# Attention and feed-forward as one program: second norm and first gate-and-up blocks between the last tiles' steps

## The chip, the core and the metric

The kernel runs on one core of one Trainium2 chip. The core has a matrix engine (TensorE, PE in the profile; its weight loads are PEld), a vector engine (VectorE, DVE), a scalar engine (ScalarE, ACT), GpSimd (POOL) and SyncE (SP), which here only issues DMAs. Each engine works through its own queue in order and waits on semaphores. The metric is device time in microseconds for one execution; lower is better.

## The reference

One transformer layer over `x` of shape (4, 256, 512): four sequences of 256 tokens, 512 channels.

```
mod = silu(c) @ wmod -> sa, ca, ga, sb, cb, gb     # six rows of 512 for each of the 4 sequences
ga, gb: sign kept, magnitude at least 0.25
h = layernorm(x) * (1 + ca) + sa
q, k, v = h Wq, h Wk, h Wv; rope on q and k         # 32 heads, 8 key heads, head size 128
dt = softplus(h Win + bias); G = cumsum(-dt * exp(A)) in chunks of 128
y = (q k^T * exp(G_i - G_j), lower triangle) (v dt) + (q exp(G)) state of the chunk before
y = y / rms(y) * gnorm * silu(h Wg)
x = x + ga * (y Wo)
h = layernorm(x) * (1 + cb) + sb
x = x + gb * (silu(h Wgate) * (h Wup)) Wdown        # inner width 1376
```

## The kernel before

**Numbers.** Most products are kept near full precision by splitting both operands in a rounded part and a rest (`split_hi`, a cast, L44; `split_lo`, a subtraction, L49) and adding three products (`three_products`, L54 to L56). A block of a projection is 4 slices of the 512 channels times three products: 12 matmuls of 128 x 512 into one PSUM bank. A few products stay in plain float32.

**Three parts, two programs.** `block_attention` does everything up to the residual `x1 = x + ga * attention`; `block_ffn` holds two blocks of its own, gate and up first, down second. Between these three blocks every engine waits for all others. The token axis is 8 tiles of 128 (`t`, two to a sequence) or two halves of 512.

**Prologue of the attention.** The rows `sa` and `ca` come from `mod_row` (L588): 4 matmuls with a stationary operand of 4 columns, added up in PSUM, then copied and turned into columns (`mod_turn`, L597). First norm (`Norm`), first key and value projection, and four steps t = -4 to -1 that project queries (`q_block`) and gates (`g_block`) for the first half. Among them are the softplus chain on VectorE (semaphore `chain`), the cumulated decays (`cumulative`, L626 to L632), their store to DRAM and the broadcast load back into `dec` (`load_dec`, L445), which ScalarE awaits in `exp_g` (L783). GpSimd clears `x1` (L1395) once the first norm has turned its tiles. The loop's first product is `scores` (L670).

**The loop.** `groups` runs 8 groups of 4 heads over 8 tiles. A step holds scores, `q_block` and `g_block` for the next half, `y_product`, `out_product` (12 matmuls, added to `x1` by `add_out` one step later) and `square_sum`. Seven groups are a hardware loop, the last is written out.

**The last four tiles** have no projection left for the next half, so `tail(g, t)` takes the place of `step`. It fills TensorE's queue with the four remaining modulation rows (`mod_row` of GA, CB, GB, SB). VectorE bounds the gates (`guard_gate`), SP stores them, loads them back as broadcast rows (`grow`), loads `x` again, and GpSimd does `scale_tile` and `add_x` (L406, L413) for tiles 0 to 6, VectorE for tile 7. Statistics of the second norm are taken there too (`stats_of`).

**Feed-forward.** After the barrier the second norm is normalised, turned (L165), modulated by ScalarE (L175) and split; 11 slices of 128 inner channels follow, each for two halves: gate block, up block (12 matmuls each), `Silu` on ScalarE (L1561), product on VectorE (L1595), split into `a_hi` and `a_lo`. Gate and up have two PSUM banks each. The weights alternate between two buffers. After the second barrier the down projection takes 8 tiles x 11 slices x 3 matmuls, result scaled by `gb`, added to `x1` and stored.

Of the kernel before, what the change touches and what calls it, by code (L numbers as in the profile page):

```python
# [5 lines left out]
ALU = mybir.AluOpType  # L6
# [4 lines left out]
P = 128  # L11
# [4 lines left out]
EPS = 1e-5  # L16
# [12 lines left out]
POOL_TILES = 7  # L29

# [8 lines left out]
SA, CA, GA, SB, CB, GB = range(6)  # L39

# [18 lines left out]
def build(nc, x_in, cT_in, wmod_in, wq_in, wg_in, wkv_in, wo_in, win_in, rows_in, gnorm_in,  # L59
# [4 lines left out]
    with ExitStack() as outer:  # L64
        def sb(name, shape, dt=F32, side=None):
            return outer.enter_context(nc.sbuf_tensor(name, shape, dt, side=side))
# [13 lines left out]
        block_attention(nc, cst, x1, hT_hi, hT_lo, tok, modT, gnorm, ident, modrow, gT_dram,  # L80
                        x_in, cT_in, wmod_in, wq_in, wg_in, wkv_in, wo_in, win_in, rows_in,
                        gnorm_in, cst_in, wgu_in, norm_rows, raw_pair)
        block_ffn(nc, x1, hT_hi, hT_lo, modT, ident, modrow, wgu_in, wd_in, out, norm_rows,
                  raw_pair)
# [110 lines left out]
def block_attention(nc, cst, x1, hT_hi, hT_lo, tok, modT, gnorm, ident, modrow, gT_dram,  # L195
                    x_in, cT_in, wmod_in, wq_in, wg_in, wkv_in, wo_in, win_in, rows_in,
                    gnorm_in, cst_in, wgu_in, norm_rows, raw_pair):
    with ExitStack() as ctx:
        def sb(name, shape, dt=F32, side=None):
            return ctx.enter_context(nc.sbuf_tensor(name, shape, dt, side=side))  # L200
# [4 lines left out]
        def sem(name):  # L205
# [37 lines left out]
        ps_q, ps_g, ps_kv, ps_s, ps_y, ps_x, ps_ss, ps_o = (  # L243
            ps(n) for n in ("ps_q", "ps_gt", "ps_kv", "ps_s", "ps_y", "ps_x", "ps_ss", "ps_o"))
# [4 lines left out]
        silu_c = sb("silu_c", [P, KT * B])  # L249
# [7 lines left out]
            for i in range(6))  # L257
# [3 lines left out]
        wmod = {SA: qT[:, 1], CA: sg[:, 1]}  # L261
        mod_rows = sg[0:B, 0, 0:2]
        ps_rows = {SA: ps_q[0:B], CA: ps_g[0:B]}
        ps_modT = ps_o[:, 0:2 * KT * B].rearrange("p (m k b) -> p m k b", m=2, k=KT)
        ps_z, ps_glast = (ps_o[:, i * NT * H:(i + 1) * NT * H].rearrange("p (t h) -> p t h", h=H)
                          for i in range(2))
        ps_zT = ps_gT = [ps_x, ps_ss]

        wmod[GA] = raw_o
        wmod[GB] = [raw_kv[:, 0:2].rearrange("p k d -> p (k d)"),  # L270
                    raw_kv[:, 2:4].rearrange("p k d -> p (k d)"),
                    raw_q[:].rearrange("p k d -> p (k d)"), raw_g[:].rearrange("p k d -> p (k d)")]
        wmod[CB], wmod[SB] = qT[:, 0], sg[:, 0]
        late_rows = dec[0:B, 0].rearrange("p h c i -> p (h c i)")\
            .rearrange("p (m n) -> p m n", m=2)
        gates = [q_sin[0:B], tok[0:B].rearrange("p t r h -> p (t r h)")[:, 0:HID]]
        gmag = q_cos[0:B]
        ps_rows.update({GA: ps_q[0:B], GB: ps_g[0:B], SB: ps_kv[0:B], CB: ps_q[0:B]})
        ps_late_modT = ps_q[:, 0:2 * KT * B].rearrange("p (m k b) -> p m k b", m=2, k=KT)
        grow, x_again = raw_o, [qT[:, 0], sg[:, 0]]  # L280
        norm = Norm(ctx, nc, "1", norm_rows, x1, hT_hi, hT_lo, modT[:, 0], modT[:, 1], ident,
                    [ps_s, ps_y, ps_x, ps_ss], True, hf)
        norm2 = Norm(ctx, nc, "2", norm_rows, x1, None, None, None, None, None, None, True, None)
# [71 lines left out]
        small_loaded = sem("small_loaded")  # L355
        sigc_done = sem("sigc_done")
# [16 lines left out]
        gates_ready = sem("gates_ready")  # L373
# [4 lines left out]
        xa_loaded = [sem(f"xa_loaded{i}") for i in range(2)]  # L378
        scaled = [sem(f"scaled_{n}") for n in ("pool", "dve")]
        residual = [sem(f"residual_{n}") for n in ("pool", "dve")]  # L380
        block = ctx.enter_context(nc.Block())
# [10 lines left out]
        def groups(engine, step, tail):  # L392
# [5 lines left out]
            for t in range(NT):  # L398
                if t < 4:
                    step(KVH - 1, t, True, True, False)  # L400
                else:
                    tail(KVH - 1, t)
# [6 lines left out]
        def add_x(engine, queue, who, t, n):  # L409

            queue.wait_ge(scaled[who], n + 1)
            queue.wait_ge(xa_loaded[t // 4], 16)
            engine.tensor_tensor(x1[:, t], x1[:, t], x_again[t // 4][:, t % 4], ALU.add)\  # L413
                .then_inc(residual[who], 1)

        @block.sync
        def _(sp):
            def load_mod(m):
                if m == GB:
                    for k in range(KT):  # L420
                        sp.dma_start(wmod[m][k], wmod_in[m][:, k]).then_inc(mod_loaded[m], 16)
                else:
                    sp.dma_start(wmod[m][:], wmod_in[m]).then_inc(mod_loaded[m], 16)
# [33 lines left out]
            for j in range(1, GRP):  # L457
                load_head(0, j)
# [7 lines left out]
            load_o(0)  # L466

            def step(g, t, project, next_batch, next_group):
# [14 lines left out]
                if not next_group and t == 1:  # L483
                    sp.wait_ge(wo_split, KVH + 1)
                    sp.wait_ge(wo_late, KVH + 1)
                    load_mod(GA)
                    load_mod(GB)

            def tail(g, t):
                if t == 4:  # L490
                    step(g, t, False, True, False)
                    sp.wait_ge(zz_done, g * 8 + 4)
                    load_mod(CB)
                    load_mod(SB)
# [1271 lines left out]
```

## Time and profile before

| | us |
|---|---|
| median of 3 runs (lowest, highest) | 1100.27 (1097.45, 1101.43) |
| the profiled execution, as timed | 1100.45 |
| its span in the trace | 1098.7 |
| TensorE busy / VectorE / ScalarE / GpSimd | 1045.7 / 816.6 / 696.6 / 224.2 |

The profiled execution lies 0.2 us above the median. The span runs from the first to the last instruction; 1.75 us lie around it. Mean granted TensorE clock 0.979. Times below are from the start of the span. A matmul's printed duration covers its way through the array, so that neighbours overlap: what one costs in a row of them is the distance of their starts.

### The profile page before, as it was taken

How to read it: one execution, taken by the hardware profiler on the slowest of the kernel's cores; microseconds unless marked ns; L12 is line 12 of the kernel's file. 1: busy time of each engine (PE TensorE's matmuls, PEld its weight loads, DVE VectorE, ACT ScalarE, POOL GpSimd, SP SyncE). 2: the span in 40 equal slices, each digit the busy share in tenths (PEclk: the TensorE clock that was granted, in tenths of full speed). 3: DMA queues.
4: the chain of work that ended last, by engine and by line, in shares of the span. 5: the costliest groups of instructions: out<-in, count | busy, mean ns of one | idle time of the engine just before them, and what ended most of it. 6: DMA issues, size and time to landing. Idle time of an engine off the chain costs nothing. (4 is left out here: it accounts for less than half of the span.)

```text
span 1098.7 us, 14605 instructions
## 1 busy us (share of the span) xinstructions
PE 1045.7 (95%) x4680; PEld 808.4 (74%) x4680; DVE 816.6 (74%) x1585; ACT 696.6 (63%) x1368; POOL 224.2 (20%) x140
## 2 busy tenths in 40 slices
PE   5879999999999999999999999999997859999898
PEld 1657777777777777877777777787774349888786
DVE  5777887888888788878888887887878785444412
ACT  3448877887787788778878787877874434222300
POOL 3412212222211131122222112211323410000000
PEclk9989999999999999999999999999998969999999
DMA  6122301310131122013101311220123231111011
GB/s 226 55 67 80 112 20 38 100 53 19 38 115 39 33 85 91 19 38 115 38 19 38 126 44 40 77 76 19 45 72 135 76 129 45 57 38 58 29 39 38
DMA packets 37464, 70.89 MB, mean 65 GB/s; under 512 B 2936, under 2 KB 19576, under 8 KB 35520
## 3 DMA queue, kind: packets, MB, share of 16 engines
q1 hardware_dynamic: 36720, 70.16, 19.8%
q10 hardware_dynamic: 720, 0.43, 0.1%
q8 instruction: 13, 0.21, 0.1%
q14 instruction: 11, 0.09, 0.0%
HBM read 68.33 MB, written 2.24 MB: 64 GB/s over the span
## 5 line engine op out<-in xcount | busy, mean ns | idle before, releaser
L1373 POOL TENSOR_TENSOR q_sin<-q_sin,cst 128x512 f32<-128x512 f32 x64 | 88.9, 1388 | 311.7 <-ACT q_sin L764 311.7
L1213 DVE SCALAR_TENSOR_TENSOR prob<-ps_s,scal,dec 128x128 f32<-128x128 f32 x256 | 71.9, 343 | 77.6 <-PE ps_s L670 77.6
L1361 POOL TENSOR_TENSOR dec<-dec,future 128x1024 f32<-128x1024 f32 x31 | 74.5, 2402 | 265.9 <-ACT expg L783 265.9
L54 PE MATMUL ps_q<-hT_hi,wq_hi 128*128 128x512 f32 x256 | 125.5, 490 | 3.3 <-DVE q_cos L1023 2.5
L54 PE MATMUL ps_o<-wo_hi,z_hi 128*128 128x512 f32 x260 | 103.8, 399 | 2.5 <-DVE z_lo L49 2.4
L54 PE MATMUL ps_gt<-hT_hi,wg_hi 128*128 128x512 f32 x256 | 103.8, 405 | 2.0 <-DVE sg L1043 2.0
L56 PE MATMUL ps_o<-wo_hi,z_lo 128*128 128x512 f32 x260 | 103.4, 398 | 0.0
L55 PE MATMUL ps_o<-wo_lo,z_hi 128*128 128x512 f32 x260 | 103.2, 397 | 0.0
L56 PE MATMUL ps_q<-hT_hi,wq_lo 128*128 128x512 f32 x256 | 101.2, 395 | 0.0
L55 PE MATMUL ps_gt<-hT_lo,wg_hi 128*128 128x512 f32 x256 | 101.1, 395 | 0.0
L56 PE MATMUL ps_gt<-hT_hi,wg_lo 128*128 128x512 f32 x256 | 100.7, 393 | 0.0
L55 PE MATMUL ps_q<-hT_lo,wq_hi 128*128 128x512 f32 x256 | 100.4, 392 | 0.0
L805 ACT ACTIVATE sq_parts<-sq_sum 64x512 fp32r<-64x512 f32 x64 | 40.5, 633 | 65.9 <-DVE sq_sum L1232 64.3
L793 ACT ACTIVATE dec<-dec,scal 128x128 f32<-128x128 f32 x256 | 81.1, 389 | 1.3 <-DVE scal L994 1.3
L54 PE MATMUL ps_kv<-wkv_hi,hT_hi 128*128 128x256 f32 x256 | 73.1, 286 | 0.0
L55 PE MATMUL ps_kv<-wkv_lo,hT_hi 128*128 128x256 f32 x256 | 72.7, 284 | 0.0
L56 PE MATMUL ps_kv<-wkv_hi,hT_lo 128*128 128x256 f32 x256 | 72.7, 284 | 0.0
L54 PEld LDWEIGHTS ps_q<-hT_hi,wq_hi 128*128 128x128 f32 x256 | 48.5, 190 | 27.0 <-issue 17.0
L670 PE MATMUL ps_s<-qT,kT 128*128 128x512 f32 x128 | 65.8, 595 | 2.5 <-DVE qT L1031 2.5
L55 PEld LDWEIGHTS ps_q<-hT_lo,wq_hi 128*128 128x128 f32 x256 | 48.6, 190 | 22.5 <-issue 14.4
L773 ACT ACTIVATE sig<-sig 128x512 f32<-128x512 f32 x64 | 39.9, 624 | 35.9 <-DVE sig L1037 35.5
L1043 DVE SCALAR_TENSOR_TENSOR sg<-ps_gt,gnorm,sig 128x512 f32<-128x512 f32 x64 | 47.9, 748 | 18.3 <-ACT sig L775 18.2
(251 smaller groups left out, 2737.6 us busy)
## 6 DMA issues: line engine op xcount, KB each, us to landing
dec<-gT_dram SPq DMA_DIRECT2D x32, 512.0 KB, 5.5
raw_q<-wq_in SPq DMA_DIRECT2D x32, 256.0 KB, 2.7
raw_g<-wg_in SPq DMA_DIRECT2D x32, 256.0 KB, 2.9
raw_o<-wo_in SPq DMA_DIRECT2D x8, 1024.0 KB, 6.9
raw_pair<-wkv_in SPq DMA_DIRECT2D x8, 512.0 KB, 4.7
raw_pair<-wgu_in SPq DMA_DIRECT2D x6, 512.0 KB, 3.2
raw_gu<-wgu_in SPq DMA_DIRECT2D x5, 512.0 KB, 3.4
qT<-wmod_in SPq DMA_DIRECT2D x2, 1024.0 KB, 6.9
```

Of the source, the lines that this page charges most:

```text
L54: pe.matmul(out, w_hi, x_hi, start=first, stop=False)
L55: pe.matmul(out, w_hi, x_lo, start=False, stop=False)
L56: return pe.matmul(out, w_lo, x_hi, start=False, stop=last)
L670: nc.tensor.matmul(ps_s[:].rearrange("p (h i) -> p h i", h=GRP), kT[:, b % 2, c * P:(c + 1) * P], qT[:, half, :, rows_of(t)], start=True, ...
L773: nc.scalar.activation(sig[:], sig[:], ACT.Ln, bias=1.0).then_inc(lsig_done, 1)
L793: last = nc.scalar.activation(cell, cell, ACT.Exp, bias=scal[:, bn * CPB + c, 0, h:h + 1])
L805: nc.scalar.activation(sq_parts[0:64], sq_sum[:], ACT.Copy).then_inc(sqhi_done, 1)
L1043: nc.vector.scalar_tensor_tensor(sg[:, half, j], ps_g[:], gnorm[:], sig[:], ALU.mult, ALU.mult).then_inc(sg_done, 1)
L1213: last = nc.vector.scalar_tensor_tensor(prob[:, h], ps_s[:, h * P:(h + 1) * P], scal[:, tile, 1, h:h + 1], dec[:, tile // 2 % 2, h, tile % ...
L1361: nc.gpsimd.tensor_tensor(cells, cells, future[:].unsqueeze(1).broadcast_to([P, GRP * CPB, CHUNK]), ALU.add).then_inc(mask_done, 1)
L1373: nc.gpsimd.tensor_tensor(q2, q2, sinT, ALU.mult).then_inc(qsin_done, 1)
```

## The change

- One program, one block: `layer` takes the place of `block_attention` and `block_ffn`. The feed-forward's buffers are laid over attention buffers that are free by then.
- **Modulation rows**: all six are computed in the prologue. `silu_c` is padded from 4 to 32 columns, and the four matmuls of a row go to four strips of 32 PSUM partitions (`ps_rows[m][k * LANE:(k + 1) * LANE]`) instead of being added up; `mod_turn` adds the strips by 4 small matmuls with a 0/1 matrix `sel`. ScalarE copies each row out of PSUM (128 x 512). The gates are bounded on 128 x 32 elements in column form (`guard_gates`) and stored to `modrow` by two DMAs of 2048 single float32 each, on SP's queue after `load_o(0)`. The clearing of `x1` moves to t = -2.
- **Last four tiles**: `tail` is gone. A list written out by hand for each engine holds their steps, the second norm in five sets of tiles (`LN_SETS`), and the gate and up blocks e = 0, 1, 2 of the feed-forward. For these three ScalarE makes the sigmoid from exp, log and exp. The squares are taken whole and summed by a plain float32 product. `residual_tile` on GpSimd starts with tiles 0 and 1 in steps 2 and 3 of the last group.
- **Feed-forward**: the first two slices are loaded and split twice, once for each half (13 weight loads for 22 blocks). Gate and up have one PSUM bank each. ScalarE does all hi splits of the weights, GpSimd the first three lo splits, VectorE the others. The down projection begins without a barrier; ten of its weight slices' loads are spread over the last blocks.

```diff
-C_ID, C_COST, C_SINT, C_COS, C_SIN, C_TRI, C_END = 0, 128, 384, 640, 896, 1152, 1280
+C_ID, C_COST, C_SINT, C_COS, C_SIN, C_TRI, C_SEL, C_END = 0, 128, 384, 640, 896, 1152, 1280, 1288
+LANE = 32
+FIRST_W = 2
+W_ORDER = list(range(IT)) + list(range(FIRST_W))
+FFN = [(i, it, half) for i, it in enumerate(W_ORDER)
+       for half in ((0,) if i < FIRST_W else (1,) if i >= IT else (0, 1))]
+LN_SETS = ((0, 2), (2, 2), (4, 2), (6, 1), (7, 1))
...
+            def mod_rows(m):
+                pe.wait_ge(mod_loaded[m], 16)
                 for k in range(KT):
+                    nc.tensor.matmul(ps_rows[m][k * LANE:(k + 1) * LANE], silu_c[:, k], wmod[m][:, k],
+                                     start=True, stop=True).then_inc(rows_ready, 1)
...
+            sp.wait_ge(guard, GUARD_END)
+            for i in range(2):
+                sp.dma_start(modrow[i].rearrange("(m p) -> p m", p=P),
+                             gate_T[:, i].rearrange("p b k -> p (b k)"),
+                             allow_slow_non_contiguous=True).then_inc(rows_stored, 16)
...
             softplus_argument()
+            pe.wait_ge(norm.hf_done, NT)
+            mod_rows(GA)
             q_block(0, -3)
             softplus_turn()
+            pe.wait_ge(kT_done, 1)
+            mod_rows(GB)
             g_block(0, -3, 0, KT)
+            mod_turn(2)
+            mod_rows(SB)
             q_block(0, -2)
+            mod_turn(3)
+            mod_rows(CB)
             g_block(0, -2, 0, KT)
             cumulative()
+            mod_turn(4)
             q_block(0, -1)
+            mod_turn(5)
             g_block(0, -1, 0, KT)
+            pe.wait_ge(late_modT_done, 2)
...
+            scores(g, 4)
+            cross_scores(g, 4)
+            kv_chunk(g, 2, 0)
+            kv_chunk(g, 2, 1)
+            y_product(g, 4)
+            scores(g, 5)
+            out_product(g, 4)
+            square_sum_whole(g, 4)
+            y_product(g, 5)
+            ln_turn(0)
+            square_sum_whole(g, 5)
+            k_turn(g, 2)
+            scores(g, 6)
+            cross_scores(g, 6)
+            out_product(g, 5)
+            ln_turn(1)
+            scores(g, 7)
+            y_product(g, 6)
+            out_product(g, 6)
+            square_sum_whole(g, 6)
+            y_product(g, 7)
+            ffn_gate(0)
+            ffn_up(0)
+            square_sum_whole(g, 7)
+            out_product(g, 7)
+            ffn_gate(1)
+            out_product(g, 8)
+            ffn_up(1)
+            ln_turn(2)
+            ln_turn(3)
+            ffn_gate(2)
+            ln_turn(4)
+            ffn_up(2)
+            for e in range(EARLY_E, len(FFN)):
+                ffn_gate(e)
+                ffn_up(e)
+            pe.wait_ge(alo_done, len(FFN))
...
+            for e in range(EARLY_E, len(FFN)):
+                ffn_prod(e)
+                if e > EARLY_E and e == LAST_OF[i - 1] + 1 and i + 1 < len(W_ORDER):
+                    split_w_lo(i + 1)
+                ffn_lo(e)
```

TensorE's list stands in the first part, VectorE's loop over the later blocks in the last. VectorE's list between `gate(g, 3)` and `y_product(g, 5)`'s last operand is: `ln_stats(0)`, `gate(g, 3)`, `ln_stats(1)`, `gate_y(g, 4)`, `ln_variance(0)`, `probabilities(g, 5)`, `add_out(g, 4)`, `cross_probabilities(g, 4)`, `split_prob_lo(g, 5)`, `ln_normalise(0)`, `split_v_lo(g, 2)`. GpSimd's list there is `residual_tile(2)`, `split_w_lo(0)`, `residual_tile(3)`, `mask`, `split_w_lo(1)`, `ln_lo(0)`, `residual_tile(4)`, `ln_lo(1)`, `residual_tile(5)`, `split_w_lo(2)`, `residual_tile(6)`. ScalarE's begins `split_w_hi(0)`, `copy_v`, `decays(g, 5)`, `squares_whole(g, 4)`, `ln_rstd(0)`, `split_w_hi(1)`.

## Rows read from the trace of the kernel before

**Rows 1.** The page, busy time, share of the span, instructions of each engine

```profile
PE 1045.7 (95%) x4680; PEld 808.4 (74%) x4680; DVE 816.6 (74%) x1585; ACT 696.6 (63%) x1368; POOL 224.2 (20%) x140
```

**Rows 2.** Stretches: length, busy PE, PEld, DVE, ACT, POOL, granted clock, DMA

```profile
46.98:78.58 31.60, 24.58 (x100) 18.21 (x100) 22.90 (x43) 13.82 (x26) 3.84 (x3) 0.89 0.18 54
78.58:827.66 749.08, 749.08 (x3421) 587.10 (x3422) 625.79 (x1270) 593.75 (x1157) 173.41 (x98) 1.00 0.19 60
827.66:904.89 77.23, 55.36 (x179) 28.98 (x178) 61.03 (x111) 31.59 (x70) 25.26 (x16) 0.83 0.32 113
904.89:1028.99 124.10, 124.09 (x590) 105.05 (x588) 54.28 (x75) 33.70 (x60) 0.00 (x0) 0.98 0.15 49
```

**Rows 3.** Who waited for whom, PE, 827.66 to 904.89: total, times, longest

```profile
PE ps_ss L701 <- DVE sq_parts L49: 5.6, 3, 2.5
PE ps_ln L165 <- DVE xn2b L153: 4.7, 1, 4.7
```

**Rows 4.** Timeline of PE: start, duration; one modulation row, then starts of neighbouring blocks

```profile
860.53 3.60 PE L588 MATMUL ps_kv<-sg,silu_c 128*4 128x512 f32 x8
...
865.57 1.02 PE L693 MATMUL ps_x<-qT,kT 128*128 128x512 f32 x2
...
1023.38 0.39 PE L54 MATMUL ps_fg<-hT_hi,wgu_hi 128*128 128x512 f32 x1
...
1026.10 0.39 PE L54 MATMUL ps_fu<-hT_hi,wgu_hi 128*128 128x512 f32 x1
```

**Rows 5.** Groups between 827.66 and 904.89: count, busy, mean ns of one

```profile
L1213 DVE SCALAR_TENSOR_TENSOR prob<-ps_s,scal,dec 128x128 f32<-128x128 f32 x16 | 4.5, 343 | 1.1 <-PE ps_s L670 1.1
...
L124 DVE BATCH_NORM_STATS2 stats<-x 128x6 f32<-128x512 f32 x8 | 5.4, 675 | 0.0
...
L406 POOL TENSOR_TENSOR x<-x,raw_o 128x512 f32<-128x512 f32 x7 | 10.0, 1446 | 21.9 <-DVE x L1049 21.9
```

**Rows 6.** Timeline of DVE and POOL, a cast beside GpSimd's mask and one alone

```profile
843.07 2.34 POOL L1361 TENSOR_TENSOR dec<-dec,future 128x1024 f32<-128x1024 f32 x1 [18.67 <-ACT expg L783]
843.42 2.28 DVE L44 CAST prob_hi<-prob 128x512 fp32r<-128x512 f32 x1
...
871.98 0.43 DVE L44 CAST prob_hi<-prob 128x512 fp32r<-128x512 f32 x1
```

**Rows 7.** VectorE's operations on `wgu_lo`: count, duration in ns min/median/max, first and last start

```profile
L49 DVE TENSOR_TENSOR wgu_lo<-raw_gu,wgu_hi x5: 1224/1225/1226, 916.3 to 999.4; 128x1024 fp32r<-128x1024 f32 x5
```

**Rows 8.** Timeline, the second barrier: VectorE's last steps, TensorE's first

```profile
1029.09 0.69 DVE L1595 TENSOR_TENSOR prod<-ps_fu,prod 128x512 f32<-128x512 f32 x1 [3.36 <-PE ps_fu L56]
...
1030.48 0.69 DVE L49 TENSOR_TENSOR a_lo<-prod,a_hi 128x512 fp32r<-128x512 f32 x1 [0.69 <-ACT a_hi L1564]
...
1032.54 0.62 PE L54 MATMUL ps_d<-d_hi,a_hi 128*128 128x512 f32 x1 [3.56 <-PEq L1446]
```

**Rows 9.** Timeline of the prologue's last steps, all engines

```profile
41.46 3.52 POOL L1395 MEMSET x<- 128x4096 f32 x1
...
56.05 0.47 PE L54 MATMUL ps_q<-hT_hi,wq_hi 128*128 128x512 f32 x1 [2.47 <-DVE q_cos L1023]
...
62.67 0.50 PE L54 MATMUL ps_gt<-hT_hi,wg_hi 128*128 128x512 f32 x1 [2.05 <-DVE sg L1043]
...
70.59 0.39 SPq L445 DMA_DIRECT2D dec<-gT_dram  x1
...
75.34 0.63 ACT L783 ACTIVATE expg<-dec 128x512 f32<-128x512 f32 x1 [0.40 <-DMA dec<-gT_dram]
...
78.58 1.13 PE L670 MATMUL ps_s<-qT,kT 128*128 128x512 f32 x2 [2.51 <-DVE qT L1031]
```

**Rows 10.** The page's DMA queues: packets, MB, share of 16 engines' span

```profile
q1 hardware_dynamic: 36720, 70.16, 19.8%
q10 hardware_dynamic: 720, 0.43, 0.1%
```

**Rows 11.** Timeline of ACT: the first `exp_g` of the loop

```profile
95.86 0.61 ACT L783 ACTIVATE expg<-dec 128x512 f32<-128x512 f32 x1
```

More of the change, by code:

```diff
@@ L1 @@
+import math
 from contextlib import ExitStack
@@ L273, in block_attention @@
[L273 to L280, printed above, removed]
+        ps_zT = ps_gT = [ps_x, ps_ss[:]]
@@ L390, in group_slice, with groups @@
             return bass.ds(g * size, size)
-        def groups(engine, step, tail):
+        def groups(engine, step, between):
             with engine.Fori(0, KVH - 1) as g:
@@ L397, in groups @@
                     step(g, t, True, True, True)
[L398 to L402, printed above, removed]
+            for t in range(4):
+                step(KVH - 1, t, True, True, False)
+                between(t)
         def scale_sum(engine, who, t):
@@ L753, in _, with square_sum_whole, ln_turn @@
-            groups(pe, step, tail)
-            out_product(KVH - 1, NT)
+            def square_sum_whole(g, t):
+                pe.wait_ge(sq_done, g * 8 + (t + 1))
+                pe.wait_ge(lnss_done, g * 8 + t)
+                nc.tensor.matmul(ps_ss[:], ones[:].bitcast(F32), sq_whole[:], start=True, stop=True)\
+                    .then_inc(ss_ready, 1)
+            def ln_turn(s):
+                first, count = LN_SETS[s]
+                pe.wait_ge(xn2_done, first + count)
+                if s == 1:
+                    pe.wait_ge(hf2_done, 1)
+                bank = (pairs[0], pairs[0], pairs[1], ps_s[:].unsqueeze(1), ps_y[:].unsqueeze(1))[s]
+                for c in range(count):
+                    for k in range(KT):
+                        last = nc.tensor.transpose(bank[:, c, k * P:(k + 1) * P],
+                                                   xn2[:, (first + c) % 4, k * P:(k + 1) * P], ident)
+                last.then_inc(turned2, 1)
@@ new lines, in _ @@
+            groups(act, step, lambda t: None)
+            g = KVH - 1
+            split_w_hi(0)
+            copy_v(g, 2)
+            decays(g, 5)
+            squares_whole(g, 4)
+            ln_rstd(0)
+            split_w_hi(1)
+            split_prob_hi(g, 5)
+            inverse_rms(g, 4)
+            exp_g(g, 2)
+            squares_whole(g, 5)
+            ln_modulate(0)
+            copy_kT(g, 2)
+            act.wait_ge(o_ready, g * 8 + 5)
+            split_z_hi(g, 4)
+            ln_rstd(1)
@@ L957, in _ @@
+            act.wait_ge(up_ready, len(FFN))
+            for k in range(D_FIRST, IT):
+                split_d_hi(k)
         @block.vector
@@ L1706, in constants, with between @@
+            def between(t):
+                if t in (2, 3):
+                    residual_tile(t - 2)
+            groups(pool, step, between)
+            residual_tile(2)
+            split_w_lo(0)
+            residual_tile(3)
+            mask(KVH - 1, 2)
+            split_w_lo(1)
+            ln_lo(0)
+            residual_tile(4)
+            ln_lo(1)
+            residual_tile(5)
+            split_w_lo(2)
+            residual_tile(6)
 def constants():
```

1008 lines of the change are left out of this document (538 added, 470 removed).

## The prediction

> **What bounds the kernel now.** The page comes first: TensorE is busy 1045.7 of 1098.7 us, VectorE 816.6 [rows 1]. So a gain of more than a few us must come from the 53 us in which TensorE stands, or from its slow clock. The stretches say where those lie [rows 2]. In the loop (78.58 to 827.66) TensorE is busy in all 749.08 us: nothing there is touched. Between 827.66, where the tail's first `scores` starts, and 904.89, the first gate matmul, 77.23 us pass with 55.36 busy, 21.9 idle, at a mean granted clock of 0.83, a mixture of the two levels (2.4 and 1.2 GHz). The waits there [rows 3] name VectorE's short steps and the normalising behind the barrier: a chain from tile to tile with nothing to fill it. The gate and up stretch, 904.89 to 1028.99, is full again. In the prologue's last part (46.98 to 78.58) TensorE idles 7.0 us.
>
> **The tail before, in full-clock work.** One block of 12 matmuls takes 1026.10 - 1023.38 = 2.72 us, a pair of gate and up 5.44, all 22 pairs 119.7 [rows 4]. As they end at 1028.99, the tail costs 1028.99 - 827.66 - 119.7 = 81.6 us. TensorE's own work in it, from the starts in the timeline at full clock: 4 modulation rows of 3.45 (13.8) and their turns (0.6); 5 out products of 2.8 (14.0); 6 plain float32 products for scores and cross scores of 0.86 [rows 4] (5.2); 4 y products (4.5); one key and value batch (2.9); squares and key turns (1.2); the norm's turns (3.6). Together 45.8. With 21.9 idle, 13.9 are left: what the low clock cost.
>
> **The tail after.** The rows go (-14.4); the square sums become plain float32, 4 x (0.86 - 0.23) = +2.5. So 33.9 of own work, plus 16.3 for three pairs of gate and up. What waits remain I worked out by laying the four lists on one time axis from `scores(g, 4)`, each operation at its duration in the rows (four `probabilities` of 343 ns spaced 0.28 = 1.12, statistics of a tile 0.84, GpSimd's product or addition 1.3 to 1.45 [rows 5]). Of these waits, 18.5 us in all, 12.6 come in three places:
> - before `y_product(g, 5)`, 6.4. VectorE reaches `gate_y(g, 4)` at 9.2, since ScalarE does `split_w_hi(0)`, `copy_v` and `decays(g, 5)` before the squares; then probabilities, `add_out`, cross probabilities, rest of prob (13.7), `ln_normalise(0)` (16.0) and `split_v_lo` stand before it, to 16.3. TensorE had run out at 10.1.
> - before `out_product(g, 5)`, 3.6: `z_lo` is behind statistics of two tiles, a split and GpSimd's `ln_lo(0)`; it ends at 26.5.
> - before gate e = 3, 2.6: the third sigmoid by exp, log and exp comes after the last modulations, and frees the single gate bank late.
>
> The rest: 1.5 (set 3 to be normalised), 1.4 and 1.2 (before `y_product(g, 7)` and `out_product(g, 6)`), 1.1 (`kT`), 0.7 in small ones. Gate 3 starts at 33.9 + 16.3 + 18.5 = 68.7, against 81.6 + 16.3 = 97.9 before: **-29.2**. VectorE has about 47 us of work in these 68 and GpSimd 35, so they are nearly as loaded as TensorE: these waits are VectorE's order, not slack.
>
> In that axis a VectorE operation between SBUF tensors waits for GpSimd's running one, and the reverse. The row that shows it: a cast of 0.43 us alone takes 2.28 when it starts in GpSimd's mask, and ends with it [rows 6]. If they ran side by side unhindered, gate 3 would start at 60.1. The Trainium skill (SBUF — State Buffer, Terms, "shared port pair") says that the loser "fully blocks" for the whole instruction; by that rule, which speaks against moving norm work and residuals beside VectorE, and with which the row agrees, it is 68.7.
>
> **The low clock.** It cost 13.9 before with 21.9 idle; with 18.5 idle there are bounds of 0 and 11.7. Doubling TensorE's operations in the 14 us behind the first wait and the 10 us behind the second moves gate 3 by 3.9, as VectorE covers the rest: **+3.9**, the middle.
>
> **Later blocks.** With one bank each, gate e + 1 needs `Silu` of e (0.6 us, while the up block of 2.7 runs) and up e + 1 the product (0.65, while the next gate runs): covered by 2 us each. The three doubled matters are ACT's hi splits (1.04) and VectorE's rests, 1.23 each [rows 7], for 13 weights instead of 11; ACT and DVE were 34 and 54 of 124 us busy there [rows 2]. One is not covered: e = 20 is a slice with one block only; VectorE does `ffn_prod(20)`, then the rest for slice 12, which gate 21 needs: 0.65 + 1.23 + 0.4 of handing over = **+2.3**. The down projection: before, product, hi, rest and barrier held TensorE 3.56 us, then 8 matmuls at 1.2 GHz (+1.6) [rows 8]; now product, hi and rest alone, 2.4: **-2.8**. If the clock falls in these two gaps, up to 1.6 comes back each. SP's d loads are issued tens of us ahead; if not, TensorE would wait there for one of 2 to 3 us.
>
> **Prologue.** Four more rows stand in TensorE's list. The nearest row prices one at 3.45 [rows 4], whatever the stationary's width. On the timeline: GA from 46.3 to 49.8, `q_block(-3)` to 52.5 (before: 49.9), GB to 56.4, gate block 59.1, SB 62.7, `q_block(-2)` 65.4, CB 68.9, gate block 71.6, then `cumulative`. So TensorE itself, not VectorE, sets that pace, and the idle 2.47 and 2.05 [rows 9] are used up. Behind it the chain is as before: G's store, its load at 70.59, ScalarE's exp at 75.34 when it lands, `scores` at 78.58 [rows 9]. The copy of G could start at 68.3 before and at about 72.8 to 73 now: with late `modT` +0.5, **+5.1**. The other bound: four matmuls in the time of one, 0.86 + 0.15 each. Then `q_block(-2)` starts about when VectorE lets it, as before, and only the extra copies (ACT 4 x 0.6), the bounding of the gates (VectorE 5 x 0.2) and the last wait remain: +0.7. I take the upper, the row's own price. Clearing `x1` (3.52 [rows 9]) moves within the same stretch, and blocks VectorE there instead of at 42: 0 (-1.5 to +2). The first norm: TensorE's turns wait for `modT`, but VectorE takes up the first split only 0.2 us after it could: **+0.3**. `residual_tile` 0 and 1 in steps 2 and 3 of the last group: 6 us of GpSimd beside VectorE, which has 16% of each step free: **+0.5**.
>
> **The stores of the gates.** 4096 packets of 4 bytes stand in SP's queue before the `dec` load of the loop's first step. 256 per DMA engine: at the packet time of ScalarE's queue, 0.1% x 16 x 1098.7 / 720 = 24 ns, 6 us; at that of q1, whose packets hold 1.9 KB, 19.8% x 16 x 1098.7 / 36720 = 95 ns, 24 us [rows 10]. Issued at 82.9 and behind `wo` (4.8), the `dec` load (5.3) then lands at 99 or 117; ScalarE wants it at 95.86 + 5.1 = 101 [rows 11]. So 0 or +16; the packet is nearer to the small ones: 0.
>
> **Sum.** 1100.45 - 29.2 + 3.9 + 2.3 - 2.8 + 5.1 + 0.3 + 0.5 = 1080.6. The profiled execution stands 0.2 above the median.
>
> **Rivals.**
> - *Rows side by side* (33%). The same chain with the prologue's other bound: 1080.6 - 4.4 = 1076.2; with a mild clock, 1072. For it: the change gives each matmul its own strip of 32 partitions and its own start and stop, and nothing else. Against: no row shows two matmuls at once; a 4-column operand costs as much as a 128-column one. The Trainium skill (TensorEngine Tiling (Array Packing), Performance Considerations) says that a stationary side of 32 or less can be tiled 4 times by columns. By that rule the later four rows take 4 us of TensorE instead of 13.8.
> - *The tail's order is worse than laid out* (15%). In-order lists with hand-set order lose where one step is late: each lateness of VectorE is paid by TensorE. If idle and low clock stay as before (21.9 + 13.9 instead of 18.5 + 3.9), it gives +13.4: 1094; half of it 1087.
> - *The stores hold back `dec`* (5%), the case that ends on the other side: if a 4-byte write takes 0.15 us, 256 of them take 38, `dec` lands at 131, ScalarE stands 30 us in the first step and TensorE with it, since scores of the third tile need `dec`: 1111. It decides from 0.12 us per packet.
> - *The change does not do what it says*: it does by its lists; only the three pairs' place could be worthless if VectorE were the bound throughout (3%): 1100.
>
> **How the numbers follow.** The forecast has 44%. The range holds it with the first rival and the half of the second: 1069 (side by side, clock at its lower bound, 1076.2 - 3.9 = 1072.3, and the freed 3 us at 42) to 1090. Left out are the other half of the second rival, the stores and the last, near 16%. About 0.5% (5.5 us) can be told from no change. Faster by more: all but the stores, the last, and a sliver of the second: 0.92; within: 0.04; slower: 0.04.
>
> **What would show it.** Gate matmuls of e = 3 begin 65 to 73 us after the last group's fifth `scores`, with the longest waits before `y_product(g, 5)` (on VectorE), `out_product(g, 5)` and gate 3. Two gaps of 2.3 us stand before gate 21 and before the down projection. Strip matmuls in the prologue follow one another if serial, and run in the same stretch if not; the loop begins at 83 to 84 or at 79. TensorE busy stays near 1045 - 14 x (side by side) + 2.5. The forecast is wrong if the tail's idle is above 22 us, if ScalarE waits for a DMA at the first `exp_g`, or if the stretch of later blocks isn't full.

## The result, and the profile after

The changed kernel takes 1087.95 us (median of 4 runs, 1087.06 to 1089.31), the kernel before 1099.13 (4 runs of the same measurement). The ratio is 0.990, 95% interval 0.987 to 0.992: 1.0% less time. The predicted 1080.6 is 7.4 us too low; the range, 1069 to 1090, holds the result. The profiled execution took 1087.06 us with a span of 1085.3, against 1100.45 and 1098.7 before: 13.4 less on both counts. When the changed kernel ran again, one of its four executions took 2660.7 us, like no other here; the median given for it below is that of the other three.

The page's first part, beside [rows 1]: TensorE has 8.0 us less work and stands only 47.6 us.

```profile
PE 1037.7 (96%) x4668; PEld 809.6 (75%) x4668; DVE 794.3 (73%) x1556; ACT 707.9 (65%) x1381; POOL 234.9 (22%) x145
```

Stretches of the changed kernel answer to [rows 2]: the loop with steps 0 to 3 of the last group, from there to gate 3, on to the down projection, and to the end. Columns: stretch and length; busy PE, PEld, DVE, ACT, POOL with counts; granted clock; DMA share, GB/s.

```profile
83.37:843.46 760.09, 753.09 (x3421) 588.89 (x3422) 627.56 (x1269) 593.33 (x1155) 178.56 (x102) 0.99 0.20 60
843.46:909.21 65.75, 56.70 (x228) 39.20 (x226) 55.32 (x106) 40.50 (x86) 30.76 (x16) 0.94 0.29 92
909.21:1020.60 111.39, 107.12 (x457) 87.74 (x457) 39.78 (x54) 36.05 (x54) 0.00 (x0) 0.97 0.15 48
1020.60:1085.30 64.70, 60.52 (x264) 49.41 (x264) 15.73 (x24) 3.38 (x7) 0.00 (x0) 0.99 0.09 33
```

In the kernel before, the down projection starts at 1032.54 [rows 8], and gate 3 would start at 827.66 + 97.9 = 925.56 by the prediction's own count. That gives five parts:

| part | before | after | change | forecast |
|---|---|---|---|---|
| start to the loop's first scores | 78.58 | 83.37 | +4.8 | +5.4 |
| loop and the last group's steps 0 to 3 | 749.08 | 760.09 | +11.0 | +0.5 |
| `scores(g, 4)` to gate 3 | 97.9 | 65.75 | -32.1 | -25.3 |
| gate 3 to the down projection | 106.98 | 111.39 | +4.4 | +1.1 |
| down projection to the end | 66.16 | 64.70 | -1.5 | -1.6 |

The forecast's -2.8 for the down projection is split here: 3.56 - 2.4 = 1.2 lie ahead of it, and the 1.6 of low clock behind its start. The tail gave 6.8 more than forecast. Three other parts took 20 us back, where 7 had been forecast. The largest loss lies in the loop, whose own code hardly changed.

What TensorE waited for in the whole changed kernel (waits on whom: us in total, times, longest), those of the start, of the first norm and those under 2.0 left out:

```profile
PE ps_ss L820 <- DVE sq_parts L63: 7.0, 2, 3.6
...
PE ps_kv_x L731 <- issue: 3.1, 1, 3.1
PE ps_q_gt L858 <- DVE xn L1646: 2.9, 1, 2.9
PE ps_s L68 <- DVE a_lo L63: 2.2, 1, 2.2
PE ps_q_gt L68 <- DVE raw_q L1676: 2.2, 1, 2.2
PE ps_q_gt L68 <- issue: 2.0, 1, 2.0
PE ps_s L789 <- DVE modT L1427: 2.0, 1, 2.0
```

The first row is the one to see: 7.0 us before two square sums, at 113.66 in the loop and at 842.89 in the last group's step 3. [Rows 3] had that pair of names in the tail; now it stands in steps that were full before. Each of the rows got an experiment, or a reading below, but for the last: it stands before the first `scores`, was 2.51 in the kernel before [rows 9], and is 1.9 to 2.0 in the trace of every run below.

### The profile page after: what moved, and what is told of

It is laid out like the page before. It is cut to its first block, busy times and chain, and to the rows that moved or that the text cites. A ratio compares the mean times of both kernels' runs of the same rounds, so it can differ in the third digit from the quotient of the medians.

```text
span 1085.3 us, 14475 instructions
## 1 busy us (share of the span) xinstructions
PE 1037.7 (96%) x4668; PEld 809.6 (75%) x4668; DVE 794.3 (73%) x1556; ACT 707.9 (65%) x1381; POOL 234.9 (22%) x145
## 3 DMA queue, kind: packets, MB, share of 16 engines
HBM read 69.38 MB, written 2.24 MB: 66 GB/s over the span
## 4 chain that ended last, share of the span: by engine, by line
PE 84%; issue 5%; POOL 3%; DVE 3%; DMA 3%; ACT 1%; SPq 1%; POOLq 0%; DVEq 0%; ACTq 0%
PE ps_q_gt L68 13%; PE ps_q_gt L70 13%; PE ps_q_gt L69 13%; PE ps_o L70 5%; PE ps_o L69 5%; PE ps_o L68 5%; PE ps_s L789 5%; PE ps_kv_x L70 3%; PE ps_kv_x L69 3%; PE ps_kv_x L68 3%; PE ps_kv_x L812 2%; PE ps_y L798 2%; DMA dec<-gT_dram 2%; PE ps_ss L820 1%; PE ps_y L806 1%
## 5 line engine op out<-in xcount | busy, mean ns | idle before, releaser
L68 PE MATMUL ps_q_gt<-hT_hi,wq_hi 128*128 128x512 f32 x256 | 126.3, 493 | 0.0
L68 PE MATMUL ps_q_gt<-hT_hi,wg_hi 128*128 128x512 f32 x256 | 103.2, 403 | 0.0
L70 PE MATMUL ps_q_gt<-hT_hi,wq_lo 128*128 128x512 f32 x256 | 100.8, 394 | 0.0
L69 PE MATMUL ps_q_gt<-hT_lo,wg_hi 128*128 128x512 f32 x256 | 100.6, 393 | 0.0
L69 PE MATMUL ps_q_gt<-hT_lo,wq_hi 128*128 128x512 f32 x256 | 100.4, 392 | 0.0
L70 PE MATMUL ps_q_gt<-hT_hi,wg_lo 128*128 128x512 f32 x256 | 100.1, 391 | 0.0
L68 PE MATMUL ps_q_gt<-hT_hi,wgu_hi 128*128 128x512 f32 x176 | 70.3, 400 | 4.3 <-DVE raw_q L1676 2.2
L68 PE MATMUL ps_kv_x<-wkv_hi,hT_hi 128*128 128x256 f32 x256 | 74.4, 291 | 0.0
L69 PE MATMUL ps_kv_x<-wkv_lo,hT_hi 128*128 128x256 f32 x256 | 73.5, 287 | 0.0
L70 PE MATMUL ps_kv_x<-wkv_hi,hT_lo 128*128 128x256 f32 x256 | 73.4, 287 | 0.0
```

The lines of the kernel that those rows point to most:

```text
L68: pe.matmul(out, w_hi, x_hi, start=first, stop=False)
L69: pe.matmul(out, w_hi, x_lo, start=False, stop=False)
L70: return pe.matmul(out, w_lo, x_hi, start=False, stop=last)
```

## The experiments

Ten runs followed: the first four of the table on one chip, the next four on a second, the last two on a third. Medians are compared with the changed kernel's 1088.0 (1087.95); against the 1087.26 that it took when it ran again, on the first four's chip, each gain is 0.7 smaller and each loss 0.7 larger. Each ratio is to the kernel before on the same chip, with its 95% interval.

| run | us | ratio to before |
|---|---|---|
| changed kernel, again | 1087.26 | 0.988 (0.985 to 0.990) |
| gate_rows | 1080.13 | 0.981 (0.978 to 0.983) |
| residual_later | 1083.87 | 0.985 (0.983 to 0.986) |
| clear_later | 1083.89 | 0.985 (0.983 to 0.986) |
| rows_in_turn | 1093.27 | 0.994 (0.992 to 0.996) |
| pairs_behind | 1096.90 | 0.997 (0.995 to 0.998) |
| w12_first | 1085.34 | 0.987 (0.986 to 0.989) |
| gate2_silu | 1085.54 | 0.988 (0.986 to 0.990) |
| three_cures | 1074.35 | 0.977 (0.975 to 0.980) |
| all_cures | 1068.77 | 0.973 (0.970 to 0.975) |

**The mark, the changed kernel again.**

> The changed kernel once more, as the mark that the other three of this set are read against. Every theory: 0.99 of the kernel before, near 1088 us.

It came out at 0.988, 1087.26 us. Its trace shows how far two executions of one kernel differ: the first `scores` comes at 81.98 in place of 83.37, since the clock did not fall behind the wait before the cumulative sum (3.06 there, 3.10 in the changed kernel's trace), and the wait before the square sum in the loop is 5.41 us in place of 3.63.

**gate_rows: the stores of the gates.**

```diff
-            sp.wait_ge(guard, GUARD_END)
-            for i in range(2):
-                sp.dma_start(modrow[i].rearrange("(m p) -> p m", p=P),
-                             gate_T[:, i].rearrange("p b k -> p (b k)"),
-                             allow_slow_non_contiguous=True).then_inc(rows_stored, 16)
+            sp.wait_ge(gates_copied, 1)
+            sp.dma_start(modrow.rearrange("i (m p) -> (i m) p", p=P), gate_rows[:]).then_inc(rows_stored, 16)
...
+            nc.tensor.transpose(ps_ss[0:2 * B * KT, 0:P], gate_T[:].rearrange("p m b k -> p (m b k)"),
+                                ident).then_inc(gates_turned, 1)
```

> The gate vectors leave as 32 rows of 512 bytes in one transfer, turned on TensorE and copied out of a PSUM bank that is free by then, in place of 4096 elements of 4 bytes in two. Theory: the small elements hold the queue, so the decay of the next batch lands late, the exp of decay waits 4.3 us for it, and TensorE waits 3.6 us before the square sum of step 0 and runs at the low clock behind that. Without them both go: 3 to 6 us less than the changed kernel, and scores(0,0) to scores(7,4) 755 us in place of 760. Rival: the first steps are late because the prologue leaves TensorE at the low clock and VectorE with a backlog, and the transfers only look long: under 1.5 us less, and the wait before the square sum of step 0 stays over 2.5 us.

Measured: 7.9 us less (7.1 against the repetition), more than expected. SyncE's queue (start, duration of the issue) in the changed kernel, then in this one:

```profile
82.18 4.32 SPq L555 DMA_DIRECT2D modrow<-gate_T  x2
86.88 0.55 SPq L524 DMA_DIRECT2D dec<-gT_dram  x1
87.69 1.69 SPq L507 DMA_DIRECT2D raw_q<-wq_in  x1
89.48 8.36 SPq L509 DMA_DIRECT2D raw_g<-wg_in  x1
```

```profile
81.50 0.43 SPq L557 DMA_DIRECT2D modrow<-gate_rows  x1
85.90 0.40 SPq L527 DMA_DIRECT2D dec<-gT_dram  x1
86.56 0.35 SPq L510 DMA_DIRECT2D raw_q<-wq_in  x1
87.01 0.38 SPq L512 DMA_DIRECT2D raw_g<-wg_in  x1
```

Two issues of 4-byte elements hold SyncE 4.32 us. The last line's issue, 8.36 here, takes 7.5 to 9.7 in four of the eight traces with these stores, and 0.38 in the other four, so it isn't what costs. The `dec` load is issued 4.7 us behind the start of the stores, and in gate_rows 4.4: the held queue isn't it either. From issue to landing, the changed kernel's table of transfers (last column, us) reads, and below it that of gate_rows:

```profile
dec<-gT_dram SPq DMA_DIRECT2D x1, 512.0 KB, 19.7
...
modrow<-gate_T SPq DMA_DIRECT2D x2, 8.0 KB, 17.2
```

```profile
dec<-gT_dram SPq DMA_DIRECT2D x1, 512.0 KB, 5.6
```

So it is the landing: `dec` lands at 86.88 + 19.7 = 106.6, and ScalarE, which takes it at 101.64 in gate_rows, stands 4.3 us for it. ScalarE's exp of the decay and its copy for the square sum, then TensorE's square sum, in the changed kernel:

```profile
106.73 0.63 ACT L983 ACTIVATE expg<-dec 128x512 f32<-128x512 f32 x1 [4.32 <-DMA dec<-gT_dram]
```

```profile
113.66 0.47 PE L820 MATMUL ps_ss<-sq_parts,ones_r 128*128 128x512 f32 x1 [3.63 <-DVE sq_parts L63]
113.97 1.24 PE L789 MATMUL ps_s<-qT,kT 128*128 128x512 f32 x2
115.00 1.92 PE L812 MATMUL ps_kv_x<-qT,kT 128*128 128x512 f32 x2
```

The last line takes 1.92 us where it takes 1.02 in gate_rows: the clock fell to its lower level behind the wait (granted clock 0.84 in 109:120, 1.00 in gate_rows). The stretch 100:120 in the changed kernel, and in gate_rows:

```profile
100.00:120.00 20.00, 16.37 (x60) 11.53 (x60) 15.36 (x30) 12.38 (x24) 3.90 (x3) 0.91 0.32 87
```

```profile
100.00:120.00 20.00, 20.00 (x84) 15.34 (x84) 18.55 (x38) 16.85 (x34) 5.15 (x3) 1.00 0.32 105
```

Full, and at clock 1.00. The rival asked for a wait still over 2.5 us; none is left. From the first `scores` to the last group's fifth it is 754.34 us in place of 760.09, as expected (755). That is 5.8; the medians' 7.9 fits a wait that is longer in other executions (3.3 to 7.7 us in the eight traces with these stores). Two things set it. `dec` lands 19.3 to 22.1 us after its issue. And ScalarE comes to it 19.0 us behind the first `scores` where the clock fell there (the product behind it takes 1.9 us), 17.3 where it didn't (1.02). The four traces with 19.0 have waits of 3.3, 3.6, 3.8 and 5.6 us, the four with 17.3 have 5.3, 5.4, 7.3 and 7.7, each four in the order of the landing. Why the landing varies stays open.

**residual_later: two residual tiles on GpSimd.**

```diff
-                if t in (2, 3):
-                    residual_tile(t - 2)
+                if t == 3:
+                    residual_tile(0)
+                    residual_tile(1)
```

> Residual tiles 0 and 1 both go behind step 3 on the POOL queue, in place of one behind step 2 and one behind step 3. Theory: residual tile 0 holds the rotation q_sin on POOL for 3.2 us, so the q add of the last projection is late and TensorE idles 3.4 us at 842.9 and runs at the low clock behind it: that goes, 3 to 6 us less than the changed kernel. Rival: TensorE waits there for something that comes late anyway (the scores of step 4 need the same kT and the same VectorE queue), or the wait returns one step further, where POOL now does two tiles together: within 1.5 us of the changed kernel.

Measured: 4.2 us less (3.4 against the repetition). Its four executions all lie below the repetition's three (1080.2 to 1084.7 against 1086.3 to 1088.8), though the intervals of the ratios touch. GpSimd's timeline in the changed kernel:

```profile
834.86 1.48 POOL L487 TENSOR_TENSOR x<-x,raw_o 128x512 f32<-128x512 f32 x1
836.41 1.63 POOL L494 TENSOR_TENSOR x<-x,raw_q 128x512 f32<-128x512 f32 x1
838.00 1.29 POOL L1811 TENSOR_TENSOR q_sin<-q_sin,cst 128x512 f32<-128x512 f32 x1
```

VectorE's, behind it, and TensorE's, behind that:

```profile
839.40 1.67 DVE L1346 TENSOR_TENSOR qT<-q_cos,q_sin 128x512 f32<-128x512 f32 x1 [2.52 <-POOL q_sin L1811]
```

```profile
842.89 0.77 PE L820 MATMUL ps_ss<-sq_parts,ones_r 128*128 128x512 f32 x1 [3.37 <-DVE sq_parts L63]
```

The residual tile stands in GpSimd's order ahead of a rotation that is on the path. With the tiles behind step 3, the rotation starts at 832.23, the q addition at 834.18, TensorE's square sum follows without a wait, and `scores` of steps 3 and 4 lie 837.01 - 825.83 = 11.18 us apart in place of 15.00. Part of it returns, as the rival said: a wait of 1.8 us opens within a `y_product`, and the tail takes 66.94 in place of 65.75. By the starts that leaves 3.8 - 1.2 = 2.6. The profiled execution, 1080.19, is the fastest of the four by 3.5 us.

**clear_later: the memset of `x1`.**

```diff
                     pool.wait_ge(rows_ready, KT * len(MODS))
+                    pool.wait_ge(guard, GUARD_END)
```

> The memset of x on POOL waits for the guarded gates, so it no longer stands beside the end of the softplus series on VectorE. Theory: the memset holds the one VectorE operation that took 2.48 us in place of 0.43 and two more at 1.2 to 1.9, and TensorE waits 3.1 us for their result before the cumulative sum: 2 to 3 us less than the changed kernel, first scores at 81 us in place of 83.4. Rival: the memset only moves and holds VectorE's dec mask and the q add of the last block instead (at 76 to 82 us), or what the cumulative sum gains is waited for again at the dec load: within 1 us, and first scores at 83 us.

Measured: 4.1 us less (3.4 against the repetition; here too no execution overlaps, and the intervals touch), more than expected. GpSimd's memset and VectorE's step beside it in the changed kernel, then VectorE's same step here:

```profile
64.46 3.52 POOL L1834 MEMSET x<- 128x4096 f32 x1
```

```profile
65.64 2.48 DVE L1403 TENSOR_SCALAR raw_o<-raw_o 128x256 f32<-128x256 f32 x1
```

```profile
65.12 0.29 DVE L1403 TENSOR_SCALAR raw_o<-raw_o 128x256 f32<-128x256 f32 x1
```

An operation of 0.29 us takes 2.48 and ends as the memset ends (68.12 and 67.98), on the chain for which TensorE's cumulative sum waits. That wait shrinks from 3.1 to 0.9, and the first `scores` comes at 79.73 in place of 83.37. Of these 3.6 us, 2.2 are the wait, 0.5 were there before it, and most of the rest is the clock, which in the changed kernel's trace fell behind the wait (granted clock of 60 to 79.7: 0.91 there, 1.00 here; the second cumulative product takes 1.86 us there, 1.06 here). It didn't fall in every trace: the seven with this wait have their first `scores` at 81.98 to 83.37, so the edit is worth 2.3 to 3.6 there. It is [rows 6] again, though not every operation is held: one of 128x256 on `raw_o` that starts at 65.30, inside the memset, takes 0.43 us, as it does alone (0.42 in this run).

**rows_in_turn: modulation rows one after the other.**

```diff
-                    nc.tensor.matmul(ps_rows[m][k * LANE:(k + 1) * LANE], silu_c[:, k], wmod[m][:, k],
-                                     start=True, stop=True).then_inc(rows_ready, 1)
+                    nc.tensor.matmul(ps_rows[m][0:LANE], silu_c[:, k], wmod[m][:, k],
+                                     start=k == 0, stop=k == KT - 1).then_inc(rows_ready, 1)
```

> The modulation rows' matmuls all accumulate into the lowest strip of 32 partitions, one after the other, as in the kernel before; the rest of the changed kernel stays (the turning takes that strip alone). Theory: side by side the four matmuls of a row cost about 1.0 us and in turn 3.45 us, so GA, GB, SB and CB, which now stand among the projections, cost 2.4 us more each: 5 to 10 us more than the changed kernel, less what the 3.1 us wait before the cumulative sum takes up. Rival: the prologue is paced by the transfers of the modulation weights and by VectorE's chain, so TensorE's rows are hidden either way: under 2 us more.

Measured: 5.2 us more (6.0 against the repetition), at the low end of what was expected. The edit also puts `sa` and `ca`, at the start, in turn. Its turns of a row read 32 partitions in place of 128, and take 1.05 us each where the changed kernel's take 0.95 to 1.05. TensorE's timeline (start, duration): one row in the changed kernel, and the same row in turn:

```profile
52.46 1.06 PE L694 MATMUL ps_kv_x<-sg,cross 128*32 128x512 f32 x8
```

```profile
54.66 3.62 PE L694 MATMUL ps_kv_x<-sg,cross 128*32 128x512 f32 x8
```

The four strips do run side by side, and the row is done 3.4 times as fast. Four later rows cost 10.2 us more in turn; TensorE is then busy without a break from 46.98 to 86, the wait before the cumulative sum is gone, and the first `scores` comes at 89.07, 5.7 later.

**pairs_behind: the three gate and up pairs.** They stand behind `ln_turn(4)` on TensorE, and their exp, sigmoid, product and split steps behind the norm's on the other engines; two hi splits of weights move with them on ScalarE, and GpSimd's last lo split goes behind its last residual tile.

```diff
-            ffn_gate(0)
-            ffn_up(0)
             square_sum_whole(g, 7)
             out_product(g, 7)
-            ffn_gate(1)
             out_product(g, 8)
-            ffn_up(1)
             ln_turn(2)
             ln_turn(3)
-            ffn_gate(2)
             ln_turn(4)
-            ffn_up(2)
+            for e in range(EARLY_E):
+                ffn_gate(e)
+                ffn_up(e)
```

> The first three pairs of gate and up blocks stand behind the last turn of the second norm's first half, with their steps on ScalarE and VectorE behind the norm's; the norm's steps stay among the last tiles' steps. Theory: the pairs are what TensorE does while the last tiles' chain (squares, inverse rms, z) runs on ScalarE and VectorE; without them these waits open again: 8 to 16 us more than the changed kernel, at 1096 to 1104 us, and the clock of the stretch from scores(7,4) to gate 3 falls under 0.9. Rival: the early norm alone brought the gain and the pairs only move work from behind the stretch into it: within 3 us of the changed kernel.

Measured: 8.9 us more, which leaves a gain of 0.3% over the kernel before. Gate 3 starts at 923.10, 76.67 us behind `scores(g, 4)` in place of 65.75. TensorE's timeline shows what opened:

```profile
886.43 2.07 PE L846 MATMUL ps_ss<-sq_whole,ones_r 128*128 128x512 f32 x2 [2.38 <-ACT sq_whole L1146]
...
893.34 0.47 PE L68 MATMUL ps_o<-wo_hi,z_hi 128*128 128x512 f32 x1 [1.54 <-DVE z_lo L63]
...
899.42 0.90 PE L858 MATMUL ps_s<-cst,xn 128*128 128x128 f32 x4 [2.18 <-DVE xn L1643]
901.50 1.11 PE L858 MATMUL ps_y<-cst,xn 128*128 128x128 f32 x4 [1.19 <-DVE xn L1643]
...
910.54 0.47 PE L68 MATMUL ps_q_gt<-hT_hi,wgu_hi 128*128 128x512 f32 x1 [0.58 <-DVE raw_q L1673]
```

The clock up to the first gate matmul (846.43 to 902.27) is 0.87. The pairs are the filling, and 8.9 of the net 11.2 us hang on them. In the stretch itself they are 10.9 of the 32.1 us: the other 21 remain without them, and come with the rows moved out (14.4 of TensorE's work by the prediction's count) and the norm set among the steps, which no run here takes apart.

**w12_first: the last slice's split.**

```diff
+                if i + 1 == len(W_ORDER) - 1:
+                    split_w_lo(i + 1)
                 ffn_prod(e)
```

and the same for `split_w_hi` ahead of `ffn_silu`.

> The split of the thirteenth slice of the gate and up weights stands ahead of silu(20) and prod(20) on ScalarE and VectorE, in place of behind them. Theory: TensorE's 2.0 us wait before gate 21 at 1011.05 is the low half of that split, late by its place in VectorE's order, and the low clock of the next blocks (0.82 in 1011:1020.6) is set off by it: 2 to 4 us less than the changed kernel. Rival: the wait for prod(20) behind it (2.2 us before down at 1020.6) only grows by what is gained: within 1 us.

Measured: 2.7 us less by the medians; the intervals of the two ratios overlap, so the runs alone don't tell it from nothing. The trace does: the wait of 2.03 before gate 21 is gone, and from gate 3 to the down projection it is 1017.38 - 909.87 = 107.51 us in place of 111.39. TensorE's two waits in the changed kernel, and the one left:

```profile
1011.05 0.47 PE L68 MATMUL ps_q_gt<-hT_hi,wgu_hi 128*128 128x512 f32 x1 [2.03 <-issue]
1020.60 0.50 PE L68 MATMUL ps_s<-d_hi,a_hi 128*128 128x512 f32 x1 [2.24 <-DVE a_lo L63]
```

```profile
1017.38 0.50 PE L68 MATMUL ps_s<-d_hi,a_hi 128*128 128x512 f32 x1 [2.24 <-DVE a_lo L63]
```

A wait of 2.03 cost 3.9: the clock does the rest (0.82 in 1011.05:1020.60 of the changed kernel). From gate 21 to the down projection it is 9.6 us in eight of the nine traces with this wait, and 8.0 in pairs_behind, where the clock did not fall behind it. In this run the wait behind the stores was 7.7 us, which may hide part of the gain in the time.

**gate2_silu: the third pair by Silu, and one turn moved.**

```diff
-            ln_turn(0)
             square_sum_whole(g, 5)
+            ln_turn(0)
...
-            ffn_exp(2)
+            ffn_silu(2)
             ln_modulate(4)
             split_w_hi(3)
-            ffn_sigmoid(2)
```

(with `ffn_cap(2)` and `ffn_gated(2)` left off VectorE's list).

> Two small edits. The third pair's activation is one Silu on ScalarE in place of exp, cap and sigmoid steps through VectorE, and the square sum of tile 5 stands ahead of the norm's turn 0 on TensorE. Theory: TensorE waits 2.2 us before gate 3 for VectorE's product of the second pair, held by the cap and gated steps of the third, and 2.9 us before turn 0 on VectorE's normalised row, which the square sum can fill in part: 2 to 4 us less than the changed kernel. Rival: VectorE is the bound of this stretch whatever the order, and the Silu's table load on ScalarE costs as much as it saves: within 1 us.

Measured: 2.5 us less by the medians, again within the intervals. The wait before turn 0 falls from 2.87 to 1.07, but 0.69 opens before the square sum in front of it and 0.72 before the key turn behind it; that before gate 3 falls only from 2.23 to 1.83, now on the norm's own `hT_lo`. So VectorE's norm steps are nearly as late as the third pair's. `scores(g, 4)` to gate 3 takes 64.53 in place of 65.75, and 0.8 of these 1.2 us lie ahead of the edit, in the first `scores` at a better clock. Neither theory nor rival is shown.

**three_cures and all_cures.** The edits that gained, together: first gate_rows, residual_later and clear_later, then with w12_first and both edits of gate2_silu.

> The gate vectors stored as rows of 512 bytes, residual tiles 0 and 1 behind step 3, and the memset of x behind the gates, together. Theory: the three waits lie in three places (before the first scores, before the square sum of step 0, before the scores of step 3 of the last group), so their gains (0.7, 0.4 and 0.4% of the time, measured alone) add: 14 to 17 us less than the changed kernel, 1071 to 1074 us. Rival: they share one cover, the clock and VectorE's backlog at the loop's start, and two of them together give little more than the larger: 1077 us or more.

> The same three, and the thirteenth slice's split ahead of silu(20), the third pair by one Silu, and the square sum of tile 5 ahead of turn 0. Theory: two more places behind the others, each 2 to 3 us alone: 4 to 6 us less than with the first three, 1066 to 1070 us. Rival: with the earlier waits gone the stretch of the last tiles is bound by VectorE and the later edits give under 2 us more: 1070 us or more.

Measured: 1074.35 and 1068.77. The single gains of the three are 7.9 + 4.2 + 4.1 = 16.2 (13.9 against the repetition), and together 13.7 less than 1088.0, just short of the expected 14 to 17: they nearly add, and the rival's 1077 or more didn't come. The other edits bring 5.6 more, near the sum of their two medians (2.7 and 2.5). In the two traces 3.9 of it is gate 21's wait with the clock behind it, and 1.1 lies in the tail. Against the kernel before it is 2.7% in place of 1.0%. The stretch from the first `scores` to the last group's fifth, in all_cures:

```profile
80.12:829.12 749.00, 749.00 (x3421) 587.09 (x3422) 625.69 (x1269) 592.94 (x1155) 176.48 (x100) 1.00 0.20 61
```

It is full, and as long as before the change (749.08 [rows 2]). So the loop's +11.0 was its two waits and the low clock, behind them and behind the first `scores`.

## Why the prediction was right in range and 7 us off

The measured parts miss their forecasts by -0.6, +10.5, -6.8, +3.3 and +0.1 us in the order of the table. That they sum to 6.5 is in good part luck: the loop's loss and the tail's gain were both missed, with opposite signs.

- **The tail** (-29.2 + 3.9): right in kind, too small. By the timeline, TensorE idles 9.05 us between `scores(g, 4)` and gate 3, where I had 18.5. It is busy 56.7, where I had 50.2 of work and 3.9 for the low clock. The mean granted clock of 0.94 means, by my estimate, 0.12 of the 65.75 us at the lower level, and half of that lost: 3.9, as forecast; so the work itself was 2.6 too small in my count. The step that failed is the wait of 6.4 before `y_product(g, 5)`: I had put `split_v_lo` ahead of it, which makes the values of the next batch and isn't needed there. Measured are 1.05 before it, and 2.87 before the norm's first turn behind it. The 3.6 before `out_product(g, 5)` didn't come. The 2.6 before gate 3 did: 2.2. pairs_behind confirms that the pairs fill waits, for a third of the stretch's gain.
- **The stores of the gates** (0, bounds 0 and +16): the failed step that cost most. Of the two packet times I took the lower. By my own sum (issue at 82.2, `wo` 4.8, `dec` 5.3) a landing at 106.6 leaves 14.3 us for 256 elements on each engine: 56 ns an element, midway between my 24 and 95. `dec` landed 4.3 us behind ScalarE's need, and not 16. But 4.3 us late became a wait of 3.6, 5.8 in the stretch with the low clock behind it, and 7.9 in the medians: I had put nothing on a wait that short. Worst, the rival built on it needed 0.12 us a packet "to decide", while its loss grows from any lateness on.
- **Residual tiles in steps 2 and 3** (+0.5): a step that failed. I costed GpSimd's 6 us by VectorE's spare share, and not by GpSimd's own order, in which the rotation of the last projection stands behind them. Every queue that a moved step passes has to be looked at: 4.2 us.
- **The prologue** (+5.4): the sum nearly right, +4.8, and all its terms wrong; the sum is luck, and the sign I had named for rows in turn, a loop that begins at 83 to 84, came with rows side by side. They ran as the rival with 33% had it. What filled the sum were the memset, costed at 0 (-1.5 to +2), for which clear_later gives back 2.3 to 3.6 in the first `scores`; a first norm later by 1.5 to 2.4; and turns of the modulation of 0.95 to 1.05 us, which I had costed at 0.15. In the norm, TensorE's two turns take 1.87 and 1.85 us (TensorE's timeline below), where the one of before took 0.65, and the first tile's turn comes at 20.22 in place of 18.01. Double durations are what the low clock gives elsewhere; the granted clock reads 1.00 in this stretch (16.25:24.00), so the cause isn't shown. The serial reckoning was off too: rows_in_turn has its first `scores` at 89.07, +10.5, and 3.6 of the 5.1 above my figure are four more turns at 1.05 in place of 0.15.

```profile
16.25 1.87 PE L702 MATMUL ps_s<-sel,z 128*128 128x4 f32 x8
17.98 1.85 PE L702 MATMUL ps_s<-sel,expg 128*128 128x4 f32 x8
20.22 1.09 PE L181 MATMUL ps_s<-cst,x 128*128 128x128 f32 x4 [0.40 <-issue]
```

- **The rival "rows side by side"** (1076.2) had its mechanism right and its time wrong, as it took the other terms over from the forecast. The Trainium skill's rule (TensorEngine Tiling (Array Packing), Performance Considerations), 4 times by columns, agrees with 3.62 / 1.06 = 3.4 here.
- **Later blocks** (+2.3, -2.8): the gaps are where I put them, 2.03 and 2.24. I left the clock out of the sum (up to 1.6 behind each, I wrote). It fell behind the first (w12_first shows it at 3.9 with it), not behind the second (granted clock 1.00 in 1020.60:1026.00), and behind the tail's last wait, before gate 3, which I hadn't thought of: 1.6 more. That is the +3.3.
- **VectorE beside GpSimd**: the Trainium skill's shared port rule (SBUF — State Buffer, Terms) speaks of a block for the whole instruction, and the 2.48 us beside the memset agrees. I had applied it to the memset too, and taken its old place and its new for equal: at its new place what it held stood on the chain that TensorE waits for.

The signs I had named did their work: ScalarE's wait for a DMA at the first `exp_g` was written down as what would make the forecast wrong, and it was there.

What the low clock costs isn't the same in every execution. Behind the wait of 2.2 us before gate 3 the granted clock is 0.64 in the changed kernel's trace (909.21:914.00) and 1.00 in that of residual_later (903.95:909.00), and from gate 3 to gate 21 it is 101.8 us in five traces with such a wait (1.8 to 2.3 us) and 100.2 in three. A difference of 1.6 us between two traces can be that and no more.

Open are how the +11.0 in the loop splits between the clock and the waits, and why the stores' landing varies. The first norm's lateness was read from the trace and not tested.

## What to carry to other kernels

A change that moves work off a tail pays in the places to which it is moved: list for each moved step the queue it now stands in, and what stands behind it there, the DMA queue and GpSimd above all. A single wait of 2 to 4 us of TensorE cost up to about twice itself here (2.03 cost 3.9), in the executions in which the clock fell behind it; so short waits are worth removing one by one, and three small edits gave about as much as the whole change (13.7 us against 11.2, or 13.2 where it ran again). Fill a chain of short dependent steps with work that is ready; turn a vector on TensorE before storing it rather than send it by elements.

## What the hardware showed that I had not expected

- A store of 2 x 2048 elements of 4 bytes: 4.32 us of issue on SyncE, landing after 15.2 and 19.2 us with a 1 MB load of 4.9 us ahead of it, the next 512 KB load 19.7 in place of 5.6. The same 16 KB as 32 rows of 512 bytes: issued in 0.43 us, landed after 4.6.
- Four float32 matmuls of 32 stationary columns on four strips, 512 wide: 1.06 us together, 3.62 in one strip.
- Four float32 matmuls (8 in the profile) of a 128-partition operand by 4 columns: 0.95 to 1.05 us, and of a 32-partition operand 1.05, where the operand of 4 partitions took 0.65.
- A VectorE operation of 0.29 us beside a GpSimd memset: 2.48 us; another, begun 0.34 us earlier beside the same memset: 0.43, as alone.
- The same wait of TensorE is followed by the lower clock in some executions and not in others: 1.6 us behind the wait before gate 3.
